# Attention's row maxima as a stream of 512-query chunks, on two fp32r pieces with two heads in 64-row tiles

## What is computed

```python
qkv = x @ W_qkv + b_qkv                    # per head: q, k, v of 16 columns
q, k = rope(q), rope(k)                    # pairs of columns rotated by position
att = einsum('bhqd,bhkd->bhqk', q, k) / sqrt(16)
att = where(causal, att, -1e9)
att = softmax(att, axis=-1)                # exp(att - max over keys) / sum
y = einsum('bhqk,bhkd->bhqd', att, v)
out = y @ W_proj + b_proj                  # then residual, layer norm, experts
```

## Time and profile before

| | |
|---|---|
| median of 3 runs | 1561.61 us (1558.49 to 1567.87) |
| profiled execution: its own time | 1565.56 us |
| profiled execution: span from first to last instruction | 1563.8 us |
| busy over the span: TensorE / VectorE / ScalarE / GpSimd | 1339.1 / 1167.3 / 799.7 / 276.2 us |
| mean granted TensorE clock | 0.899 of 2.4 GHz |
| HBM read and written | 82.98 and 48.38 MB |

### The profile page before, as it was taken

How to read it: one execution, slowest core, us unless ns; L and a number is a source line. 1 busy time by engine, 2 the same in 40 slices (tenths; PEclk the granted TensorE clock), 3 DMA queues, 4 the chain that set the end, 5 groups by cost and what they waited for, 6 DMA issues and landing times. The chain is left out here.

```text
span 1563.8 us, 26808 instructions
## 1 busy us (share of the span) xinstructions
PE 1339.1 (86%) x7840; PEld 655.1 (42%) x7840; DVE 1167.3 (75%) x2833; ACT 799.7 (51%) x1130; POOL 276.2 (18%) x282
## 2 busy tenths in 40 slices
PE   6766299899999998998998998999947765999997
PEld 3433111233333233332332332332236655999997
DVE  6997499898897797986996896880036754888886
ACT  3443100366665565665665665668825443545452
POOL 3554500001001001011001001011123331121112
PEclk9887555799999999999998999999978876999999
DMA  4587592001201201102112113000045623333420
GB/s 163 174 192 228 155 140 36 2 29 29 82 29 54 58 29 56 55 28 79 33 50 79 29 37 83 8 9 14 14 149 167 214 78 98 101 100 114 137 95 23
DMA packets 117980, 126.96 MB, mean 81 GB/s; under 512 B 14428, under 2 KB 100447, under 8 KB 117856
## 3 DMA queue, kind: packets, MB, share of 16 engines
q1 hardware_dynamic: 114272, 116.97, 26.4%
q0 software_dynamic: 3584, 8.47, 1.5%
HBM read 82.98 MB, written 48.38 MB: 84 GB/s over the span
## 5 line engine op out<-in xcount | busy, mean ns | idle before, releaser
L622 ACT ACTIVATE probs<-scores 128x1024 f32<-128x1024 f32 (+3 forms) x640 | 540.7, 895 | 415.7 <-PE scores L524 414.8
L669 DVE TENSOR_REDUCE part_max<-ring 128x1 f32<-128x512 f32 x768 | 484.5, 685 | 34.1 <-PE ring L552 32.2
L552 PE MATMUL ring<-k_stack,q_stack 96*128 96x512 bf16 (+3 forms) x1280 | 433.8, 383 | 64.7 <-DMA k_stack<-pieces_d 29.9
L524 PE MATMUL scores<-q_stack,k_stack 99*128 99x512 bf16 (+3 forms) x1280 | 344.1, 358 | 12.4 <-ACT probs L622 6.3
L542 PE MATMUL out_p<-probs,v_s 128*32 128x512 f32 (+3 forms) x2560 | 306.9, 552 | 9.3 <-POOL probs L714 5.5
L664 DVE CUSTOM_DVE_ANT_0 scratch<-ring,mask_s 128x384 f32<-128x384 f32 (+3 forms) x512 | 229.6, 488 | 100.9 <-issue 88.2
L552 PEld LDWEIGHTS ring<-k_stack,q_stack 96*128 96x128 bf16 x1280 | 120.5, 99 | 418.0 <-DVE part_max L669 170.3
L714 POOL TENSOR_SCALAR_AFFINE_SELECT probs<-probs 128x512 f32<-128x512 f32 x128 | 81.2, 634 | 865.6 <-ACT probs L622 865.6
L524 PEld LDWEIGHTS scores<-q_stack,k_stack 99*128 99x128 bf16 x1280 | 114.0, 100 | 169.9 <-ACT probs L622 67.6
L195 PE MATMUL psP<-xT,wqk_s 128*128 128x512 f32 x128 | 72.4, 731 | 34.5 <-ACT xT L234 30.7
L542 PEld LDWEIGHTS out_p<-probs,v_s 128*32 128x32 f32 x2560 | 51.6, 109 | 112.4 <-issue 90.5
(11 more groups left out here) (116 smaller groups left out, 1455.6 us busy)
## 6 DMA issues: line engine op xcount, KB each, us to landing
w_whole<-w SPq DMA_DIRECT2D x16, 1024.0 KB, 6.3
q_stack<-pieces_d SPq DMA_DIRECT2D x192, 64.0 KB, 2.7
k_stack<-pieces_d SPq DMA_DIRECT2D x192, 64.0 KB, 2.8
v_d<-vt SPq DMA_DIRECT2D x8, 1024.0 KB, 4.4
v_s<-v_d SPq DMA_DIRECT2D x8, 1024.0 KB, 6.0
o_d<-o_s SPq DMA_DIRECT2D x32, 256.0 KB, 2.1
p_o<-o_d SPq DMA_DIRECT2D x8, 1024.0 KB, 6.0
slots_d<-no_row SPq DMA_DIRECT2D x1, 5200.0 KB, 30.3
```

The lines of the kernel that those rows point to most:

```text
L524: last = nc.tensor.matmul(scores[p][:, hh, off:CHUNK], k_stack[i][0:KROWS, j, kb * P:(kb + 1) * P], q_stack[i][0:KROWS, j, c * CHUNK + off ...
L552: nc.tensor.matmul(ring[m % 3][:, 0:w], q_stack[i][0:SROWS, j, qt * P:(qt + 1) * P], k_stack[i][0:SROWS, j, t * CHUNK:t * CHUNK + w], star ...
L622: nc.scalar.activation(probs[n % 2][:, 2 * p:2 * p + 2, off:CHUNK], scores[p][:, :, off:CHUNK], ACT.Exp, scale=SCALE).then_inc(exp_done[p], 1)
L669: nc.vector.tensor_reduce(out, ring[m % 3][:, 0:w], axis=AX.X, op=ALU.max).then_inc(ring_read, 1)
```

## The change

In the projection the pieces become two: `hi` and `low` in fp32r (4 bytes; TensorE takes it in one pass), low = raw - hi on GpSimd. ScalarE's `cut_mid` and VectorE's `rest` go. A wait on `low_ready` keeps `raw` until it has been read.

In attention the product has three terms, 3 x 16 = 48 rows, and with two rows for the maximum 50 (KROWS). The stacks hold even heads in partitions 0 to 49 and odd heads in 64 to 113, so the two heads of a pair lie in different 64-row tiles of the array. The maxima no longer run unit by unit: `max_items` lists them by query chunk, 3 down to 0, with the turn of each finished chunk placed three items into the next one's; 156 items for a unit, of which eight hold two heads of 128 columns (an add of the mask, then a reduction), 48 are masked alone, 96 plain, and four are turns. The stream runs LEAD = 76 items ahead of the steps throughout, also across units. A chunk's maxima are folded, turned as fp32 rows, cut into two pieces by VectorE after the turn, and moved by four DMAs; a score step waits only for its own chunk's rows. P·V runs two steps behind the scores (LAG) with four `probs` buffers. The rows of ones come by DMA in place of a memset. DMA counts for the stacks stay at twelve per chunk, of 64 KB.

```diff
-TERMS = [(0, 0), (0, 1), (1, 0), (1, 1), (0, 2), (2, 0)]
+TERMS = [(0, 0), (0, 1), (1, 0)]
-NPIECE = 3
+NPIECE = 2
+HALF = P // 2
+NPAIR = HPU // 2
...
-        hi = [sb(f"hi{i}", [P, QKG, CHUNK], BF16) for i in range(2)]
-        mid = [sb(f"mid{i}", [P, QKG, CHUNK], BF16) for i in range(2)]
-        low = [sb(f"low{i}", [P, QKG, CHUNK], BF16) for i in range(2)]
+        hi = [sb(f"hi{i}", [P, QKG, CHUNK], F32R) for i in range(2)]
+        low = [sb(f"low{i}", [P, QKG, CHUNK], F32R) for i in range(2)]
...
-                if g:
-                    rest(b, c, g - 1)
...
-                pool.wait_ge(mid_ready, QKG * n + g + 1)
-                nc.gpsimd.tensor_tensor(low[i][:, g, :], rots[i][:, g, :], mid[i][:, g, :],
+                pool.wait_ge(hi_ready, QKG * n + g + 1)
+                nc.gpsimd.tensor_tensor(low[i][:, g, :], raw[i][:, g, :], hi[i][:, g, :],
...
+NPROB = 4
+LAG = 2
+def max_items():
+    items, fold_after, turn_at = [], {}, {}
+    for at, c in enumerate(ORDER):
+        block = []
+        for t in range(c, -1, -1):
+            for qt in range(TPC * c, TPC * (c + 1)):
+                w = (qt + 1) * P - t * CHUNK if t == c else CHUNK
+                if w == P:
+                    block += [(qt, t, half, 2, w, True) for half in range(2)]
+                else:
+                    block += [(qt, t, j, 1, w, t == c) for j in range(HPU)]
+        before = ORDER[at - 1]
+        block.insert(3, before)
+        turn_at[before] = len(items) + 3
+        items += block
+        fold_after[len(items) - 1] = c
+    return items, fold_after, turn_at
+LEAD = TURN_AT[NCH - 1] + 10
...
-        q_stack = [sb(f"q_stack{i}", [P, HPU, T], BF16) for i in range(2)]
+        q_stack = [sb(f"q_stack{i}", [P, NCH, NPAIR, CHUNK], F32R) for i in range(2)]
...
-        probs = [sb(f"probs{i}", [P, HPU, CHUNK]) for i in range(2)]
+        probs = [sb(f"probs{i}", [P, HPU, CHUNK]) for i in range(NPROB)]
...
+            def score_pair(u, i, n, p):
+                c, kb, off = STEPS[n]
+                pe.wait_ge(exp_done[p], NSTEP * u + n)
+                for hh in range(2):
+                    rows = slice(hh * HALF, hh * HALF + KROWS)
+                    last = nc.tensor.matmul(scores[p][:, hh, off:CHUNK],
+                                            k_stack[i][rows, kb // TPC, p, kb % TPC * P:(kb % TPC + 1) * P],
+                                            q_stack[i][rows, c, p, off:CHUNK],
+                                            start=True, stop=True)
+                last.then_inc(scores_ready[p], 1)
...
+            def step(u, i, uses, n, ahead, behind):
+                first, stop = PLAN[n]
+                second = min(first + 2, stop)
+                items(u, i, uses, first, second, ahead)
+                chunk_waits(u, n)
+                for p in range(2):
+                    score_pair(u, i, n, p)
+                items(u, i, uses, second, stop, ahead)
+                if behind:
+                    pv_step(*behind)
...
+                if heads > 1:
+                    first = scratch[:, j, 0:heads * w].rearrange("p (h w) -> p h w", h=heads)
...
+                    nc.vector.tensor_tensor(first, ring[m % 3][:, 0:heads * w].rearrange("p (h w) -> p h w", h=heads),
+                                            mask_s[:, CHUNK - P:CHUNK].unsqueeze(1).to_broadcast([P, heads, P]),
+                                            ALU.add).then_inc(ring_read, 1)
+                    dve.wait_ge(ring_read, NRING * u + m + 1)
+                    nc.vector.tensor_reduce(part_max[:, qt, j:HPU:2, t], first, axis=AX.X,
+                                            op=ALU.max).then_inc(pair_read, 1)
...
+            def cut_maxima(c, u, m):
+                turned = ring[m % 3][0:NMAXROW, 0:P]
+                dve.wait_ge(ring_full, NRING * u + m + 1)
+                dve.wait_ge(max_loaded[c], 1 + MAX_DMAS * u)
+                nc.vector.tensor_scalar(max_rows[c][0][:], turned, -1.0, None, ALU.mult).then_inc(max_hi_ready[c], 1)
+                dve.wait_ge(max_hi_ready[c], u + 1)
+                nc.vector.scalar_tensor_tensor(max_rows[c][1][:], turned, -1.0, max_rows[c][0][:],
+                                               ALU.mult, ALU.subtract).then_inc(ring_read, 1)
```

More of the change, by code:

```diff
@@ L382, in max_plan @@
+ITEMS, FOLD_AFTER, TURN_AT = max_items()
+NRING = len(ITEMS)
+NMAXROW = HPU * TPC
+assert NRING % 3 == 0
+LEAD = TURN_AT[NCH - 1] + 10
+def max_plan():
+    cost = [0.7 if isinstance(item, int) else 0.08 + 0.08 * item[5] + item[3] * item[4] * (1 + (item[3] > 1)) / 960
+            for item in ITEMS]
+    width = [CHUNK - off for _, _, off in STEPS]
+    plan, m, seen, done = [], LEAD, 0, 0.0
+    for w in width:
         seen += w
         start = m
-        while m < NMAX and sum(jobs[:m + 1]) - early <= seen / total * (sum(jobs) - early) + 1e-6:
+        while m < LEAD + NRING and done + cost[m % NRING] <= seen / sum(width) * sum(cost) + 1e-6:
+            done += cost[m % NRING]
@@ L385, in max_plan, with attention @@
             m += 1
-        plan[n] = range(start, m)
-    assert m == NMAX
+        plan.append((start, m))
+    assert m == LEAD + NRING
     return plan
 PLAN = max_plan()
[L393 to L398, removed]
+def attention(nc, pieces_d, v_d, causal, ident, o_d):
@@ L600, in _ @@
-            pe.wait_ge(const_loaded, 32)
-            maxima(0, 0, 1, range(NMAX))
-            turn_maxima(0)
-            maxima(1, 1, 1, range(EARLY))
-            pe.wait_ge(ones_set, 2)
-            pe.wait_ge(max_loaded[0], 16 * NPIECE)
-            score_step(0, 0, 0)
+                slot = ring[m % 3][:, 0:heads * w]
+                rows = slice(j % 2 * HALF, j % 2 * HALF + SROWS)
+                for h in range(heads):
+                    pair = j // 2 + h
+                    last = nc.tensor.matmul(slot[:, h * w:(h + 1) * w],
+                                            q_stack[i][rows, qt // TPC, pair, qt % TPC * P:(qt % TPC + 1) * P],
+                                            k_stack[i][rows, t, pair, 0:w], start=True, stop=True)
@@ new lines, in max_item, with turn_maxima, maxima @@
+                last.then_inc(ring_full, 1)
+            def turn_maxima(c, u, m):
+                pe.wait_ge(folded[c], u + 1)
+                pe.wait_ge(ring_read, NRING * u + m - 2)
+                nc.tensor.transpose(ring[m % 3][0:NMAXROW, 0:P], row_max[c][:], id_s[:]).then_inc(ring_full, 1)
+            def maxima(u, i, uses, first, stop):
+                for m in range(first, stop):
+                    if isinstance(ITEMS[m], int):
+                        turn_maxima(ITEMS[m], u, m)
+                    else:
+                        max_item(u, i, m, uses)
@@ L607, in _ @@
+            pe.wait_ge(const_loaded, 16 * 2)
+            maxima(0, 0, 1, 0, LEAD)
+            pe.wait_ge(ones_loaded, 16 * 2 * 2 * NPIECE)
+            for n in range(LAG):
+                step(0, 0, (1,), n, True, None)
             with pe.Fori(0, UNITS // 2 - 1) as k:
-                unit(2 * k, 0, (k + 1, k + 1), 2)
-                unit(2 * k + 1, 1, (k + 1, k + 2), 2)
-            unit(UNITS - 2, 0, (UNITS // 2, UNITS // 2), 1)
-            unit(UNITS - 1, 1, (UNITS // 2, None), 0)
+                unit(2 * k, 0, (k + 1, k + 1), True)
+                unit(2 * k + 1, 1, (k + 1, k + 2), True)
```

333 lines of the change are left out of this document (149 added, 184 removed).

## The result

The changed kernel takes 1634.73 us (median of 4 runs, 1629.71 to 1645.81); the kernel before, on the same chip, 1561.04 us (1558.49 to 1567.87). The ratio is 1.0475, 95% interval 1.0408 to 1.0541: slower by 4.7%, where 1402 us was forecast. The profiled execution took 1631.4 us.

What follows compares the result with a forecast made beforehand. VectorE's floor, with TensorE close before, was to bound the changed kernel: attention 44 + 1 + 7 x 97 + 50 + 35 = 809 against 951, projection 18 less, 1565.6 - 142 - 18 = 1406, so 1402 us; range 1355 to 1480.

Steps and rivals of the forecast that it cites:

- projection: Projection stage: without ScalarE's cuts and VectorE's subtractions it gains 18 us, bounds 0 and 25.
- lead-in: Maxima before the first score step: 44 us on VectorE in place of 96, plus 1 us for added waits.
- what runs side by side: Two heads' score or maximum matmuls in separate 64-row tiles: full overlap, 0.22 us per pair.
- Chunk 3's rows: Rival: chunk 3's maxima rows arrive late by DMA, four us a unit, 1432 us in all; chance 0.15.
- The tail: Unit 7's steps 20 to 39, without maxima, where ScalarE decides: 35 us.
- 97: Period per unit in the steps: VectorE's floor of 90.3 us plus 7%, bounds 92 and 104.
- The rival that had the kernel slower: Granted clock falls, array held at 1.2 GHz: 141 us a unit, 1732 us in all; chance 0.07.
- at 1.2 GHz TensorE would have no idle time at all, and after dense work the clock was full in unit 7: Argument against a falling clock in the units, the rival given chance 0.07.
- the stall of the earlier trace: Between one unit's maxima and the next's: 2.7 us, read as a wait on VectorE, expected to go.
- the fold's round trip: Fold and turn of maxima between VectorE and TensorE: three items of cover would remove the 2.7 us stall.
- 7% over the floor: Excess of a unit's period over VectorE's floor, for ring and narrow steps: 90.3 becomes 97 us.
- The floor of 90.3: VectorE's work per unit after the change, 90.3 us, some 2 higher than before.

Runs made afterwards that it cites:

- one_tile: Changed kernel with both heads of a pair in the same 64-row tile, one after the other, so nothing overlaps; 2225.86 us, ratio 1.4286.
- full_rows: Like `one_tile`, but stacks have all 128 rows, zeros where there is no data (scores 128 rows, maxima 96); 1601.69 us, ratio 1.0266.
- unrolled: Changed kernel with TensorE's and VectorE's loops over the units written out; 1556.29 us, ratio 0.9943.
- stream_bf16_unrolled: Changed kernel's order on the earlier kernel's bf16 operands and projection, with TensorE's and VectorE's unit loops written out; 1518.25 us, ratio 0.9723.
- scores_twice_unrolled: Changed kernel with every score matmul issued twice and TensorE's and VectorE's unit loops written out; 1497.80 us, ratio 0.9588.
- stream_bf16: Changed kernel's order with the earlier kernel's operands and projection (bf16, six terms, one head at a time); 1578.94 us, ratio 1.0106.
- scores_twice: Changed kernel with each score matmul issued twice, the second overwriting the same result; 1555.46 us, ratio 0.9979.

## Why the prediction was wrong

**Right: projection, lead-in, what runs side by side.** The projection's stage became 18.1 us shorter (forecast 18); VectorE's busy time there fell from 141 to 116 us. The lead-in is 45.5 us (forecast 44 + 1). A pair of 64-row tiles takes 0.23 us (forecast 0.22). Chunk 3's rows are not late: in the unit from 637.8 us TensorE has no idle time ahead of a score matmul:

```profile
L547 PE MATMUL scores<-q_stack,k_stack 50*128 50x512 f32 (+3 forms) x162 | 31.5, 444 | 0.0
```

The tail is 43 us, 8 more than the 35 forecast. One term carries the miss: 126.0 in place of 97, 29.0 x 7.5 = 218 of the 225 us between 1406 and 1631.4.

**Failed: the clock.** The sum had no term for it. The rival that had the kernel slower was the right one, and was given 7%. The step that failed is the argument against it: "at 1.2 GHz TensorE would have no idle time at all, and after dense work the clock was full in unit 7". That assumes that a busy TensorE is enough for the clock. `one_tile` shows the opposite (98% busy, clock 0.50), and `full_rows` shows what was missing (0.97 with 96 and 128 rows in use). Dense work in unit 7 of before was work on 99 and 128 rows; the row says nothing on 50. The rival's price was mis-sized as well: the array is not held at 1.2 GHz throughout (141 us a unit, 1732 us) but alternates, 126 us and 1635. Two pairs of runs raise the clock, with the loops kept or left out: 125.9 - 116.0 = 9.9 us a unit, and 116.3 - 107.9 = 8.4. Both are more likely too low than too high, for the doubled matmuls take TensorE's time themselves; what they cost was not measured. The low windows' 115 us, 15 a unit, hold part of the loops' stalls. An estimate without either comes from the units of `unrolled`: 109.7 us at a clock of 0.92, 125.8 at 0.74. The straight line through the two meets full clock near 102.5, which puts the clock's price at 116.3 - 102.5, some 14 us a unit.

The Trainium skill (TensorE: Matmul & The Clock Gate, Part 1: The HAM clock gate) has the gate set by "how busy the PE has been recently". `one_tile` disagrees with that, if busy means that TensorE has a matmul under way: 98% busy, clock 0.50. With busy read as the share of the array at work the two agree in the steps; the lead-ins at 0.50 fit as well, if the time without a new matmul counts.

**Failed: the stall of the earlier trace rows.** It was read as a wait for the fold's round trip, because the row names VectorE as TensorE's releaser, and was taken off the sum. VectorE's own row beside it has "issue" as the cause (3.22 us at 388.12). It is the turn of the loop, it stays, and `unrolled` puts its price at 9.6 us a unit (125.9 - 116.3) with what hangs on it. The Trainium skill (Runtime: NRT & Kernel Launch, Instruction fetch mechanics) says that a taken branch to a place outside the fetched window stalls the engine until its instructions are there. The runs agree as far as the stall goes away with the branch; no run here shows the fetch itself.

**Failed: 7% over the floor.** Near full clock and without loop ends a unit still takes 107.9 us. The floor of 90.3 was near (92.5 measured); what the 7% had too small is the waiting for a ring of three slots, some 14 us. That is 107.9 - 97 = 10.9 us a unit at most. `stream_bf16_unrolled`, without overlap, takes 108.7, but the doubled scores fill the time that the overlap frees, so the two say nothing of what that time buys. By the estimate above the overlapped kernel would take 102.5 at full clock: then this term is 5.5 us, and the freed time buys about 6, part of it because VectorE has 2 to 3 us less to do than on bf16.

Together, going from 125.9 to 97 by way of 116.3 (`unrolled`) and 107.9 (`scores_twice_unrolled`): 9.6 for the loops' ends, 8.4 for the clock, 10.9 for the pace. That these make the whole miss follows from the way they are formed and proves nothing; with the estimate they are 9.6, 14 and 5.5. The three causes are shown, the split between clock and pace is not.

**Open.** Why the new order loses twice as much at the loops' ends as the old one was not tried. The pauses of over 2.2 us on TensorE add up to 20 us in the kernel before and 33 in `stream_bf16`, so of 29 and 61 us gained a part is what follows a pause. A likely cause, only argued: one loop end holds both VectorE and, through turns and ring, the whole stream, and a low clock follows the pause in the timeline (0.50 from 656 to 658 us in `stream_bf16`, whose stall ended at 655). Nor was it tried whether less than a doubled score matmul would hold the clock, or whether it is the rows or the height of the row tile that counts.

## What to carry to other kernels

A change that lets small matmuls overlap in row tiles saves time on TensorE and also takes work out of the array. Read the granted clock per stage, and ask how many rows each matmul fills, before counting the saved time as a gain; if another engine is the bound anyway, the overlap has little to win and the clock to lose. When one engine's stall names another as its releaser, look at that engine's own row before crediting the stall's removal to a dependency. The word "issue" there is a hint and no proof: here it stood for a loop's turn in one place and most likely for a wait for the ring in another, and only writing out the loops told them apart.

## What the runs showed of the hardware

- Rows of zeros count as work: 96 and 128 rows mostly of zeros beside 48 and 50 rows, otherwise the same matmuls, gave a clock of 0.97 against 0.50 in the steps, and 1602 against 2226 us.
- Useless matmuls can pay: doubled scores took 79 us off with the loops in place and 58 without them.
- A kernel whose steps sit between the clock's two levels also spreads more: the executions of the kernels with 0.77 to 0.95 there lie 0.8 to 2.2% apart (1539.1 to 1573.8 us for `unrolled`, 1547.3 to 1563.6 for `scores_twice`), those of the kernels with 0.50 or at least 0.97 only 0.1 to 0.6% (1496.1 to 1500.3 for `scores_twice_unrolled`).
- Writing out the loops of two engines over the units (eight for VectorE, or seven in the old order, and six for TensorE) gained 29 to 78 us; no cost of it shows in the times.
